# Attention head average: in one of a row tile's four slots the TensorE product takes over all four heads instead of three

## What is computed

```python
q = (h @ wq.T + bq_).reshape(bh, sl, H, DH)
k = (h @ wk.T + bk_).reshape(bh, sl, H, DH)
scores = jnp.einsum('blhd,bmhd->bhlm', q, k) * inv_sqrt_d
w_avg = jax.nn.softmax(scores, axis=-1).mean(axis=1)
new_w = jax.nn.softmax(CSCALE * w_avg + rel[None], axis=-1)
sa = jnp.einsum('blm,bme->ble', new_w, h)
h1 = _ln(h + sa, l1w, l1b)
```

## Time and profile before

| | |
|---|---|
| median of 3 runs | 2105.95 us (2104.12 to 2106.22) |
| profiled execution | 2107.55 us, span 2105.7 us |
| TensorE busy over the span | 1794.7 us, 85% |
| VectorE busy | 1658.0 us, 79% |
| ScalarE busy | 1617.9 us, 77% |
| GpSimd busy | 1222.4 us, 58% |
| granted TensorE clock, mean | 0.952 |

### The profile page before, as it was taken

How to read it: one execution, slowest core, us unless ns; L and a number is a source line. 1 busy time by engine, 2 the same in 40 slices (tenths; PEclk the granted TensorE clock), 3 DMA queues, 4 the chain that set the end, 5 groups by cost and what they waited for, 6 DMA issues and landing times. The chain is left out here.

```text
span 2105.7 us, 41779 instructions
## 1 busy us (share of the span) xinstructions
PE 1794.7 (85%) x9958; PEld 1338.0 (64%) x9958; DVE 1658.0 (79%) x4049; ACT 1617.9 (77%) x5245; POOL 1222.4 (58%) x2106
## 2 busy tenths in 40 slices
PE   1788988888889888888998589659994999999996
PEld 0576766666666666666777457246662777777775
DVE  2898999899989988989999332668885777777773
ACT  1798998789888988889989224389971788888884
POOL 1266777666667666667767434349883554444450
PEclk9999999999999999999999689769997999999999
DMA  2222222122112221212220220112222000000000
GB/s 77 76 76 75 75 89 72 71 72 86 67 68 87 76 69 68 89 67 70 90 73 31 83 98 30 31 50 101 91 80 78 1 1 2 1 1 1 1 1 21
DMA packets 75345, 120.96 MB, mean 57 GB/s; under 512 B 10536, under 2 KB 59952, under 8 KB 67872
## 3 DMA queue, kind: packets, MB, share of 16 engines
q1 hardware_dynamic: 65920, 109.91, 14.9%
q10 hardware_dynamic: 7920, 5.60, 1.0%
q0 software_dynamic: 1248, 2.59, 0.4%
HBM read 95.44 MB, written 24.20 MB: 57 GB/s over the span
## 5 line engine op out<-in xcount | busy, mean ns | idle before, releaser
L441 ACT ACTIVATE a_prob<-a_scores,a_negmax 128x256 f32<-128x256 f32 x1536 | 706.7, 487 | 116.7 <-DVE a_negmax L543 66.3
L543 DVE TENSOR_REDUCE a_negmax<-a_scores 128x2 f32<-128x512 f32 x768 | 518.8, 676 | 54.8 <-PE a_scores L677 50.8
L689 PE MATMUL a_heads<-a_prob,a_diag 128*128 128x256 f32 x1920 | 483.4, 392 | 27.4 <-POOL a_diag L332 27.3
L332 POOL TENSOR_TENSOR a_diag<-ident,a_rowinv 128x256 f32<-128x256 f32 (+1 forms) x384 | 277.8, 728 | 283.7 <-DVE a_rowinv L597 252.5
L689 PEld LDWEIGHTS a_heads<-a_prob,a_diag 128*128 128x128 f32 x1920 | 362.5, 197 | 85.3 <-POOL a_diag L332 38.5
L677 PE MATMUL a_scores<-a_spread,a_spread 72*128 72x256 bf16 x1536 | 270.5, 278 | 121.1 <-ACT a_prob L441 70.5
L441 ACT ACTIVATION_READ_ACCUMULATOR a_prob<-a_scores,a_negmax 128x1 f32 x1536 | 337.8, 220 | 0.0
L677 PEld LDWEIGHTS a_scores<-a_spread,a_spread 72*128 72x128 bf16 x1536 | 124.5, 98 | 254.0 <-ACT a_prob L441 157.4
L1474 DVE TENSOR_TENSOR_SCAN c_state<-c_decay,c_psD 128x1024 f32<-128x1024 f32 x64 | 146.1, 2285 | 35.6 <-PE c_psD L1591 35.0
L1307 POOL TENSOR_TENSOR c_du<-c_state,c_c_row 128x1024 f32<-128x1024 f32 x64 | 151.3, 2366 | 30.0 <-DVE c_state L1474 20.7
L1932 ACT ACTIVATE d_prob<-d_psS,d_bias,d_inv 128x128 f32<-128x128 f32 (+1 forms) x256 | 122.1, 487 | 27.7 <-DVE d_bias L2066 27.3
(11 more groups left out here) (295 smaller groups left out, 4122.2 us busy)
## 6 DMA issues: line engine op xcount, KB each, us to landing
a_spread<-a_split SPq DMA_DIRECT2D x48, 576.0 KB
a_spread<-a_split SPq DMA_DIRECT2D x144, 192.0 KB
a_split<-a_parts SPq DMA_DIRECT2D x48, 384.0 KB
c_c_row<-c_rows SPq DMA_DIRECT2D x32, 512.0 KB, 3.6
b_w<-in_b_w SPq DMA_DIRECT2D x1, 2816.0 KB, 14.3
a_w<-in_a_w ACTq DMA_DIRECT2D x10, 256.0 KB, 5.1
b_w<-in_b_w SPq DMA_DIRECT2D x1, 1536.0 KB, 17.3
d_wqkv<-in_d_wqkv SPq DMA_DIRECT2D x2, 768.0 KB, 5.9
```

Source lines behind the costliest of these rows:

```text
L332: g.tensor_tensor(diag[part % RING][:], ident[:].unsqueeze(1).broadcast_to([P, len(heads), P]), rowinv[part % RING][:, heads.start:heads.s ...
L441: ins = a.activation(prob[part % RING][:, c, :], psS[part % 2][:, c, :], ACT.Exp, bias=negmax[part % 2][:, c:c + 1], accum_out=rowsum[part ...
L543: v.tensor_reduce(negmax[part % 2][:, hs], psS[part % 2][:, hs, :], AX.X, ALU.max, negate=True).then_inc(s["negmax_ready"], 1)
L689: ins = p.matmul(psH[:, t, :], diag[part % RING][:, k, :], prob[part % RING][:, c, :], start=(j == 0 and k == 0), stop=(j == HG - 1 and c ...
```

## The change

`FULL` is new: in slot j = 1 of every row tile TensorE sums all four heads. j = 3 stays with three, j = 0 and 2 with two. On VectorE the sum of that slot is gone; in its place stands a wait for the slot before and a count on `sum_done`, so that the waits of others keep their numbers. The diagonals of that slot hold four matrices.

```diff
-ALONE = (1, 3)
-ADDS = QSLOTS - TPS * len(ALONE)
+FULL = (1,)
+ALONE = (3,)
+ADDS = QSLOTS - TPS * len(ALONE + FULL)
@@
 def summed(j):
-    return range(1, CH) if j in ALONE else range(1, CH, BH)
+    return range(CH) if j in FULL else range(1, CH) if j in ALONE else range(1, CH, BH)
@@
-        diag = [sb(f"diag{u}", [P, CH - 1 if u % HG in ALONE else BH, P]) for u in range(RING)]
+        diag = [sb(f"diag{u}", [P, len(summed(u % HG)), P]) for u in range(RING)]
@@ sum_a, on VectorE
                     t, j = part // HG, part % HG
+                    if j in FULL:
+                        v.wait_ge(s["sum_done"], n + RING)
+                        v.sem_inc(s["sum_done"], 1)
+                        return
                     done = s["sum_done"] if j in ALONE else s["acc_step"]
@@ sum_b
-                    v.wait_ge(s["acc_step"], m * ADDS + sum(k % HG not in ALONE for k in range(part + 1)))
+                    v.wait_ge(s["acc_step"], m * ADDS + sum(k % HG not in ALONE + FULL for k in range(part + 1)))
@@ do, on VectorE
-                    elif kind == "sum_b" and part % HG not in ALONE:
+                    elif kind == "sum_b" and part % HG not in ALONE + FULL:
```

## The result

The changed kernel takes 2118.47 us in the median of 5 runs (2114.63 to 2121.73), the kernel before 2105.18 (2104.12 to 2106.22). The ratio is 1.0054, with a 95% interval of 1.0038 to 1.0071: slower by half a per cent, 13 us by the medians and 11 by the ratio.

A forecast was written before the change was run, and what follows sets the result against it. ScalarE was taken to set the pace, TensorE second. The profiled 2107.55 us plus 7.9 for TensorE's product gave 2115.5, less 1.6 for the median 2113.9, less 2 for the clock 2112; range 2101 to 2119.

The forecast's parts named there:

- rival D: Added product unhidden in slot 4 too, or at the lower clock: 2117 to 2119 us, at most 2147; chance 0.13.
- What bounds the kernel: Steady sequence: ScalarE sets the pace, TensorE is second with 0.41 us margin at the second hidden half, VectorE waits.
- VectorE's sum at 0: Removing 96 sums of 478 ns, 46 us of VectorE's work, gains 0 because none is on ScalarE's path.
- Rival C: At part 5's first maximum VectorE is the bound, so the kernel becomes faster, 2091 us; chance 0.05.
- GpSimd at 0: Four-matrix diagonals of about 1027 ns add 0.4 us per sequence, hidden in GpSimd's idle time: cost 0.
- TensorE's 0.43 us: One added head sum costs TensorE 0.43 us, twice per sequence: hidden in slot 4, between the hidden halves in slot 0.
- Point 1: 25 ordinary sequences, nearly all in looped layers: margin covers 0.37 us, each loses 0.06, so 1.5 us.
- Point 2: Seven unrolled sequences, six in the last layer: cover 0.13 us, each loses 0.30, so 2.1 us.
- Point 3: Ten sequences where ScalarE already waits for TensorE at `a_act`: no cover, each loses 0.43 us, so 4.3 us.
- Point 4: Three sequences behind a loop's turn, margin 1.52 us, one early one and the last two: cost 0.
- The clock: Shifted sequences make one or two of seven lower-clock stretches fall away: 2 us of gain, bounds 0 to 10.9 us.
- direct price: Sum of the losses from the product between the hidden halves: 1.5 + 2.1 + 4.3 = 7.9 us.

The follow-up runs named there:

- tile 0 alone: The change made for row tile 0 only, head sums in slot 4, tile 1 left as before; 2104.59 us, 1.0 being the kernel before: 0.9983.
- seventh product: Changed kernel with the attention-weights product done twice, plus one more head-sum product between the hidden halves in slot 0; 2127.28 us, 1.0109 to the kernel before.
- the case with the sum left out: Changed kernel without TensorE taking the head over, so VectorE's sum of j = 1 is simply gone; 2105.32 us, 0.9986 to the kernel before.
- filled changed kernel: Changed kernel with TensorE doing the product of attention weights and tokens twice in its idle time; 2104.58 us, 1.0002 to the kernel before.
- filled kernel before: Kernel before with TensorE doing the product of attention weights and tokens twice; 2103.08 us, 0.9999 to the kernel before.
- tile 1: The change made for row tile 1 only, head sums in slot 0 between the hidden halves; 2113.97 us, 1.0027 to the kernel before.
- the head sums moved: Head sums of j = 1 one slot later: in the kernel before 2114.36 us, 1.0057; in the changed kernel 2106.75 us, 1.0014.

## Why the prediction was right, and where it was not

The forecast was 2112 us, with 2108 to 2116 as its own band and 2101 to 2119 as the range. Slower was right, and the range held the measured 2118.47 at its upper edge, but in part by luck. That edge was rival D's, 2117 to 2119, and D's reasons did not come true: in slot 4 the change costs nothing (0.9983 for tile 0 alone, whose ordinary looped sequence stays at 22.18 us), and where the clock had fallen ScalarE's wait grew by no more than the full-clock price (1.62 - 1.19 = 0.43 us). Of the steps:

- *What bounds the kernel* was right: ScalarE sets the pace, TensorE touches it at the second hidden half. The seventh product shows it.
- *VectorE's sum at 0* was right for the looped layers, as the case with the sum left out shows in its size. It was wrong for the last layer, where it gives 0.31 us per sequence and a wait of 0.21 us for VectorE fell away. Rival C was right about the place (part 5) and wrong about the sign it would give the whole.
- *GpSimd at 0* held. A diagonal of four takes 1039 ns against the forecast 1027.
- *TensorE's 0.43 us* was exact, 2.75 against 2.32 us. Point 1 said 0.06 for an ordinary sequence, measured 0.08. Point 2 said 0.30 for the last layer's, and the product costs 0.29 there, but VectorE's relief gives as much back, so the 2.1 us were not there. Point 3 said 0.43 for a wait that exists already, and 1.19 became 1.62; its ten waits were not a fixed set, however, seven of them belong to the clock. Point 4 said 0 behind a loop's turn, and the three distances grew by 0.7, 0.6 and 0.0 us, for a reason not traced. In sum the direct price, 7.9 us by forecast, is 6.4 in the profiled pair.
- *The clock* is the step that failed. I wrote that "in an unmoved stretch nothing in the idling changes, so I take one or two" to fall away, 2 us of gain, with bounds of 0 to 10.9 us of gain and none of loss. Moving the sequences worked in both directions. A place that idled the same 1.20 us before, at full clock, got the lower clock in looped layers 1 to 3, at 1.62 us of waiting each, and lost it in the fourth; one in the last layer fell away too. Net this is 3.3 us of loss in place of 2 of gain. The waits of `a_act` for TensorE grew like this (changed kernel, 60 to 1160 us):

```profile
ACT a_act L474 <- PE a_turn L721: 17.3, 18, 2.9
```

From 10 waits and 12.2 us to 18 and 17.3.

So of the 14.2 us between the profiled executions 6.4 are direct, 3.3 are the clock's and 4.5 lie outside what the forecast looked at. In this pair the clock is part of the loss and not most of it. That the filling removes the whole loss shows what stretches at the lower clock are worth, not that the product is free: the filled changed kernel has four where the filled kernel before has seven. Each kernel was traced once, so these shares hold for one execution of each; that the product between the hidden halves costs time rests on the timed runs, on tile 1 against tile 0 and on the seventh product. Not settled is why the stretch falls in looped layers 1 to 3 of one kernel and in the fourth of the other.

## What to carry to other kernels

Look for where the second engine's uninterrupted run of work meets the first one's schedule, and give the margin there in microseconds: work costs nothing up to the margin and its full length beyond it, whatever the shares of busy time say. The table of slots matters more than the amount: the same change was a small gain in slot 4 and a loss in slot 0, and relieving VectorE was worth next to nothing except where VectorE was on the path, in the last layer and with the head sums moved. In a kernel whose TensorE idles for a microsecond or so per sequence, any change that shifts the rhythm can add stretches at the lower clock as well as remove them; bound that term on both sides, and try filling the idle time. When two variants come out alike, count their stretches at the lower clock before calling a cost nothing.

## What was not expected of the hardware

Idle waits of TensorE of 1.20 and 0.52 us, alike to the hundredth, were followed by a granted clock of 1.00 at one time and 0.50 at another, in two layers of the same kernel as well as between two kernels. At 0.50 a run of twelve head-sum records took 4.44 us against 2.75. Doing a product of 0.9 us twice in every sequence made the slower kernel 11 us faster by the ratios, 14 by the medians.
